# A graph layer with batch norm: z in two banks, tiles held for a late turn, second-stage loads issued later

## The reference

```python
summed = segment_sum(x[src], dst)                 # 50000 x 512
aggr   = summed / max(count, 1)
h      = aggr @ W_l.T + b_l + x @ W_r.T
mu, var = mean(h, axis=0), mean((h - mu)**2, axis=0)
h_norm = relu((h - mu) * rsqrt(var + 1e-5) * gamma + beta)
out    = layernorm(x + h_norm, axis=-1)           # each row, no gain and no bias
```

## Time and profile before

| what | value |
|---|---|
| median of three runs | 2593.97 us (2590.15 to 2595.03) |
| the profiled execution, its own time | 2596.68 us |
| its span in the profile | 2594.9 us |
| busy in the span: PE, DVE, ACT, POOL | 68%, 75%, 57%, 56% |
| moved by DMA | 752.89 MB, a mean of 290 GB/s |

### The profile page before, as it was taken

How to read it: one execution, slowest core, us unless ns; L and a number is a source line. 1 busy time by engine, 2 the same in 40 slices (tenths; PEclk the granted TensorE clock), 3 DMA queues, 4 the chain that set the end, 5 groups by cost and what they waited for, 6 DMA issues and landing times.

```text
span 2594.9 us, 29629 instructions
## 1 busy us (share of the span) xinstructions
PE 1757.6 (68%) x9404; PEld 1415.7 (55%) x9404; DVE 1956.6 (75%) x3451; ACT 1471.8 (57%) x2847; POOL 1456.2 (56%) x700
## 2 busy tenths in 40 slices
PE   7899999999999999999999999996400000000000
PEld 5778778878877887787778778874200000000000
DVE  6745878888877888888788888785688666666666
ACT  4333455545554554454445445542389988888887
POOL 5354555555555555555565555554196655555564
PEclk9999999999999999999999999997755555555555
DMA  5466878887888878888788878877599999999998
GB/s 184 139 211 206 260 250 266 277 253 246 257 263 255 258 246 259 258 255 264 234 262 271 255 243 253 280 240 247 163 410 426 426 426 426 426 412 414 421 421 344
DMA packets 125533, 752.89 MB, mean 290 GB/s; under 512 B 20809, under 2 KB 20809, under 8 KB 65726
## 3 DMA queue, kind: packets, MB, share of 16 engines
q1 hardware_dynamic: 70464, 617.84, 62.1%
q0 software_dynamic: 53664, 132.51, 20.7%
q10 hardware_dynamic: 1246, 0.60, 0.1%
HBM read 515.32 MB, written 246.22 MB: 293 GB/s over the span
## 4 chain that ended last, share of the span: by engine, by line
PE 33%; DMA 32%; issue 9%; DVE 9%; ACT 8%; POOL 7%; SPq 0%; POOLq 0%; ACTq 0%; DVEq 0%
DMA out<-hx 19%; PE pd L524 7%; PE pd L526 7%; PE pd L525 7%; DMA xn<-x,gi 5%; DMA xf<-x,gi 5%; PE pz L627 3%; PE pz L629 3%; PE pz L628 3%; ACT hx L881 3%; POOL xn L1331 2%; ACT hx L891 2%; DVE x_lo L1045 2%; POOL xf L1331 2%; DMA hs<-h_scratch 1%
## 5 line engine op out<-in xcount | busy, mean ns | idle before, releaser
L524 PE MATMUL pd<-wc_hi,x_hi 128*128 128x512 f32 x1564 | 628.8, 402 | 34.8 <-DVE wc_lo L922 17.3
L1379 POOL DMA_INDIRECT h_scratch<-zz,si x156 | 308.8, 1979 | 564.5 <-ACT zz L793 506.9
L735 ACT ACTIVATE h_out<-pd 128x512 f32<-128x512 f32 x391 | 233.6, 597 | 672.3 <-PE pd L526 652.1
L526 PE MATMUL pd<-wc_hi,x_lo 128*128 128x512 f32 x1564 | 614.6, 393 | 0.0
L525 PE MATMUL pd<-wc_lo,x_hi 128*128 128x512 f32 x1564 | 612.9, 392 | 0.0
L1402 POOL TENSOR_TENSOR hx<-hx,scale_b 128x2560 f32<-128x2560 f32 (+2 forms) x91 | 439.4, 4838 | 293.3 <-DMA hx<-h_scratch 251.8
L524 PEld LDWEIGHTS pd<-wc_hi,x_hi 128*128 128x128 f32 x1564 | 295.4, 189 | 98.5 <-issue 29.9
L526 PEld LDWEIGHTS pd<-wc_hi,x_lo 128*128 128x128 f32 x1564 | 295.2, 189 | 64.7
L525 PEld LDWEIGHTS pd<-wc_lo,x_hi 128*128 128x128 f32 x1564 | 295.9, 189 | 57.9
L1331 POOL DMA_INDIRECT xn<-x,gi x156 | 264.9, 1698 | 47.7 <-issue 47.7
L881 ACT ACTIVATE hx<-hx,nm 128x512 f32<-128x512 f32 x391 | 277.1, 710 | 2.8
(11 more groups left out here) (221 smaller groups left out, 2855.0 us busy)
## 6 DMA issues: line engine op xcount, KB each, us to landing
raw<-xT_whole SPq DMA_DIRECT2D x78, 1280.0 KB
h_scratch<-h_out SPq DMA_DIRECT2D x78, 1280.0 KB
hs<-h_scratch SPq DMA_DIRECT2D x78, 1280.0 KB
hx<-x SPq DMA_DIRECT2D x78, 1280.0 KB, 20.7
hx<-h_scratch SPq DMA_DIRECT2D x77, 1280.0 KB, 15.4
out<-hx SPq DMA_DIRECT2D x77, 1280.0 KB, 18.0
xn<-x,gi POOLq DMA_INDIRECT x156
xf<-x,gi POOLq DMA_INDIRECT x156
```

Of the source, the lines that this page charges most:

```text
L524: pe.matmul(pd[i][0:n, :], hi, wc["hi"][:, kc, :], start=kc == 0, stop=False)
L526: last = pe.matmul(pd[i][0:n, :], lo, wc["hi"][:, kc, :], start=False, stop=kc == KC - 1)
L1379: pool.indirect_dma_start(out=h_dram[:, :], out_offset=by, in_=zz[:, h, :], in_offset=None, bounds_check=N + 2 * P - 1, oob_is_err=True, c ...
```

## The change

Five edits, all in the order and the placing of the work. The arithmetic stays the same.

1. **z in two banks.** The second half's product goes to px instead of pz (`z_to`). It no longer waits for ACT's copy of the first half; the next turn's transpose into px waits for the copy of the second half instead.
2. **zz twice.** `zz` gets a second buffer by the turn's parity, and the semaphores of the adds are split by parity (`s_sc[h][b]`). `copy_z` waits for the add of two turns ago; the add of the turn before is now waited for on POOL, in `add_z`.
3. **Four tiles kept.** `tiles_by` spreads 337 tiles over turns 0 to 74 and leaves four, (77,2), (77,3), (77,4) and (78,0), for turn 75 (`HELD = 4`). From turn 75 on POOL issues the gathers of the next turn ahead of the add of the turn before.
4. **The loads of stage two.** None stands in turn 74 any more. Two groups are loaded in turn 77, once all gathers have landed, four more when the last z is summed (`KEPT = 6`), two after `phase_one_done`, the ninth after `bn_ready`. The places of the nine buffers are renumbered so that the first six are free in time.
5. **The order of the sums, and of stage two's first group.** Groups 76 and 77 are read back into `h_out`, which is free by then, so their loads wait for no squares. In turns 78 to 81 DVE takes the sums of a group in front of the squares of the group before. In stage two, group 0 is normalised before group 1 is squared; the other groups keep their order.

```diff
+HELD = 4
-        zz = sr("zz", [P, 2, D], F32)
+        zz = sr("zz", [P, 2, 2, D], F32)
-        KEPT = 3
+        EARLY2, KEPT = 2, 6
+        places = (0, 1, 3, 4, 5, 6, 2, 7, 8)
+        hb = [hx[:, i, 0] for i in places]
+        z_to = (pz, px)
...
-            return min(len(later), TG * EARLY - (TG * EARLY - len(later)) * (u + 1) // (U - REACH))
+            if u >= U - REACH:
+                return len(later)
+            return TG * EARLY + (len(later) - HELD - TG * EARLY) * (u + 1) // (U - REACH)
+        def sums_of(g):
+            return h_out[:, g % 2] if isinstance(g, int) and G - 2 <= g < G else hs[:, g % 2]
...
-                    sp.wait_ge(s_sc[h], 16 * (last + 1))
-                if g >= 2:
-                    sp.wait_ge(s_a2, g - 1)
+                    for v in (last - 1, last):
+                        sp.wait_ge(s_sc[h][v % 2], 16 * (v // 2) + 16)
+                if G - 2 <= g < G:
+                    sp.wait_ge(s_st[0], stored(G))
+                    sp.wait_ge(s_st[1], stored(G - 1))
+                elif g >= 2:
+                    sp.wait_ge(s_a2, g - 1 if g < G else G - 3)
...
                 for u in turns():
                     for g, t in tiles_at(u):
                         if t == tiles_in(g) - 1:
                             after_group(g, g % 2)
-                        if g == G:
-                            load_early()
                     if sums_at(u + 1) is not None:
                         load_sums(sums_at(u + 1))
+                    if u == U - 1:
+                        sp.wait_ge(s_ge, 16 * U)
+                        for h in range(2):
+                            sp.wait_ge(s_gn[h], 16 * U)
+                            sp.wait_ge(s_gf[h], 16 * U)
+                        sp.wait_ge(s_dm, TG * G + 1)
+                        load2(0, EARLY2)
+                sp.wait_ge(s_z, 2 * U)
+                load2(EARLY2, KEPT)
...
# PE, transpose_difference and correction
                     pe.wait_ge(s_dl, 2 * u + h - 1)
+                    if h == 0:
+                        pe.wait_ge(s_ze, 2 * u)
...
-                if 2 * u + h > 0:
-                    pe.wait_ge(s_ze, 2 * u + h)
-                times_wl(pz, P, h).then_inc(s_z, 1)
+                if h == 0 and u > 0:
+                    pe.wait_ge(s_ze, 2 * u - 1)
+                times_wl(z_to[h], P, h).then_inc(s_z, 1)
...
# ACT, copy_z and stage two
-                if u > 0:
-                    act.wait_ge(s_sc[h], 16 * u)
+                if u > 1:
+                    act.wait_ge(s_sc[h][u % 2], 16 * (u // 2))
...
-                if k >= 1 and not by_vector(k - 1):
+                if k == 0:
+                    normalise(0)
+                if k >= 2 and not by_vector(k - 1):
                     normalise(k - 1)
...
# DVE
-                    if sums_at(u - 1) is not None:
+                    if u < U and sums_at(u - 1) is not None:
                         take_squares(sums_at(u - 1))
...
                     if sums_at(u) is not None:
                         take_sums(sums_at(u))
+                    if u >= U:
+                        take_squares(sums_at(u - 1))
...
# POOL
                 def add_z(u, h):
                     pool.wait_ge(s_ze, 2 * u + h + 1)
+                    if u > 0:
+                        pool.wait_ge(s_sc[h][(u - 1) % 2], 16 * ((u - 1) // 2) + 16)
...
-                    if pair_at(u - 1) is not None:
+                    held = u >= U - REACH
+                    if pair_at(u - 1) is not None and not held:
                         add_z(u - 1, 1)
                     if pair_at(u + 1) is not None:
                         gather(u + 1, 0)
                         gather(u + 1, 1)
+                    if pair_at(u - 1) is not None and held:
+                        add_z(u - 1, 1)
```

More of the change, by code:

```diff
@@ L403, in load2_x, with load2 @@
                 sp.dma_start(part_of(xb[i], k), group_of(x, k)).then_inc(s_x2[i], 16)
[L405 to L411 removed]
+            def load2(first, end):
+                for k in range(first, end):
                     load2_h(k)
```

47 lines of the change are left out of this document (21 added, 26 removed).

## The result

| | median, us | runs | ratio to before, 95% interval |
|---|---|---|---|
| before | 2594.21 (2590.15 to 2595.03) | 6 | 1 |
| after | 2575.99 (2571.78 to 2587.80) | 6 | 0.9934 (0.9914 to 0.9954) |

The change makes the kernel 18.2 us faster. The prediction was 43 us, 2551, with a range of 2537 to 2569: the direction is right, the size is not, and the time lies outside the range. The ratio's interval lies clear of 1. The profiled execution of after took 2587.80 us (span 2586.1), 11.8 us over its median and the slowest of the six; that of before stood 2.5 us over its median.

What follows compares the result with a forecast made beforehand. PE was taken to bound stage one's turns, early DMA loads the passage after them, and DMAs stage two from group 1's store. -24 - 19.2 + 0 = -43.2 us gave 2551 us; own range 2541 to 2562, 8 in 10 range 2537 to 2569.

Steps and rivals of the forecast that it cites:

- Part A: Turns 0 to 74, taken as bound by PE: -10.9 - 15.0 + 2 = -24 us.
- the two gains: Turns 0 to 74: four tiles fewer, 10.9 us less; no wait for ACT's copy before the second z, 15.0 less.
- I take off 2 us for that: Turns 0 to 74: allowance for DVE waiting for gathered rows, which have less time in shorter turns; 2 us.
- gathers set the pace: Turns 0 to 74: gathers, not PE, pace the turns, so savings return as PE's waits; 2570 us, 10%.
- Part B: Turn 75 to stage two's start: -16.0, -2.5, -1.2 us for turns 75, 76, 77, then +0.5; together -19.2 us.
- from the last z to the first scaling: End of stage one: faster order of sums eaten by the loads in front; net +0.5 us on 44.7 us.
- SP issues the load of group 75 about 7 us after turn 77 opens: Turn 77: with four loads behind it, transfers of 15.4 us end 9 to 10 us after the last z.
- rival of starved sums: Last sums: loads of groups 76 and 77 delayed by 12 us or more beyond what was set; 2563 us, 10%.
- The row of 10.3 us: Before's add of 74,1, from POOL's end to its load; used to set the last add 10.5 us after last z.
- Part C: Stage two: store of group 0 about 14 us after the start, group 1 unchanged at 31.9; 0, between -3 and +3.
- three signs of being wrong: Turn 75 opens after 1760 us, first scaling after 1850, or group 1's store to end differs from 680 by over 4.
- POOL's new wait: Turns: add wait costs nothing, landings far below 20 us; if it holds the gathers, 2627 us at 1 us excess, 4%.

Runs made afterwards that it cites:

- E6: After with POOL's old order also from turn 75 on, the add of the turn before ahead of the gathers: 2576.61 us, 0.9943 of before.
- E8: After with all early loads of stage two behind the loads for the last sums: 2566.76 us, 0.9899 of before.
- E3: After with DVE's row numbers, indices(u + 2), moved ahead of the additions that take the gathered rows: 2555.08 us, 0.9849 of before.
- E4: Before with DVE's row numbers, indices(u + 2), moved ahead of the additions that take the gathered rows: 2587.84 us, 0.9972 of before.
- E7: After with no tiles kept for turn 75 (HELD = 0): 2575.89 us, 0.9933 of before.
- E2: After with both z in pz again, all other edits kept: 2586.14 us, 0.9970 of before.
- E9: After with the moves of E3 and E8 together: 2550.16 us, 0.9824 of before.
- E12: E9 with both z in pz again: 2559.50 us, 0.9872 of before.
- E11: E9 with DVE's one_hots moved behind the second difference and x_lows(1): 2553.49 us, 0.9843 of before.
- E1: Before with the second z in px and nothing else: 2590.56 us, 0.9990 of before.
- E10: E9 with each of DVE's additions of sums and squares cut in five pieces of one tile: 2551.54 us, 0.9824 of before.

## Why the prediction was wrong, step by step

- **Part A, the two gains: right.** Forecast -10.9 and -15.0 us; the turns at their shortest went down by 26.2.
- **Part A, "I take off 2 us for that": this is the step that failed.** It was right that DVE, waiting for gathered rows, is late next, and the size was taken without working out the loop: the sum of A treats the turns as bound by PE, so that PE's saving is time. The excess rose by 29.3 us in the profile, by 19.0 and 21.5 in E6 and E8, which have the same turns. So part A gave between +3 and -7 us instead of -24. The row that misled is PE's 293.14 of 300 us busy: it was read as "bound by PE". A loop that takes as long as PE's work, give or take a microsecond, looks the same in busy time. What could have been seen is that the means of before's turns (19.61 and 22.48 us) already lay over the shortest ones (19.33 and 21.60), with 17 of 41 five-tile turns over 22.5, and that POOL waited 49.7 us for `si` in 22 turns.
- **The rival "gathers set the pace" was right** and had 10%: it gave 2570, the median is 2576, and E3 shows its mechanism (E4 points the same way). The 6 us between are about what the tail was mis-sized by. What spoke against it, that PE is idle only 2.3%, has no force where both limits are close.
- **Part B, turns 75 to 77: right.** -16.0, -2.5 and -1.2 us forecast, -16.0, -2.1 and -0.4 measured. But the kept tiles and POOL's order play no part that the time shows (E7, E6): what they shift in these turns, the tail takes or gives back.
- **Part B, from the last z to the first scaling: mis-sized**, 51.2 us instead of 45.2. The step that failed is "SP issues the load of group 75 about 7 us after turn 77 opens". It was issued 12.2 us after (1822.41 - 1810.25), and the four loads of stage two stand behind it in SP's program. Counted from the opening of turn 75 the forecast is 39.4 us and the trace has 45.0, with 43.3 to 45.9 in E2, E3, E6 and E7, whatever POOL's order and PE's tiles; in all five the first scaling follows that load by 52.4 to 54.3 us. So the four loads landed until 19 us after the last z, where 9 to 10 stood, and the last add and group 76's load had them alongside. In terms of the sum: POOL was done with the last add 1.0 us later than before (the copy stood behind ACT's squares of group 74), the add took 10.2 us from there where 7.3 were in the sum, the load 7.9 where 5 stood, and the rest went 0.8 faster. E8 shows that the four loads in front do it: without them the tail is 44.4 us. The prediction had allowed for 4 to 6 us of this. Its rival of starved sums (10%) wanted 12 us or more and did not come.
- **The row of 10.3 us was right, its use was not.** The prediction weighed a turn-taking rule from the Trainium skill ("DMA: Bandwidth & Descriptors", section on queues, rings and completion order), with an estimate of 6.4 us for the add, against the trace's 10.3, and said that the sum goes by the trace. The add took 10.2. But 10.5 us after the last z, with POOL done 3.2 us after it in before, is only 7.3 from POOL's end, between the two.
- **Part C: right in each step.** 14.0 and 31.9 us, the dip of the DMA share to 0.00 between, 678.8 to the end (680 +- 4). The groups fetched early bring 3 us at most (E8). Of the three signs of being wrong two came, turn 75 opening at 1777 us and the first scaling at 1875; the third, this time to the end, did not.
- **POOL's new wait: harmless in turns 0 to 74, as forecast, and perhaps not at the end.** It held twice in the span, both times in turn 77 with no gather behind it, ahead of the adds of 76,1 and 77,0:

```profile
1813.63 2.83 POOL L1411 DMA_INDIRECT h_scratch<-zz,si  x1 [2.26 <-DMA h_scratch<-zz,si]
1822.69 2.59 POOL L1411 DMA_INDIRECT h_scratch<-zz,si  x1 [6.22 <-DMA h_scratch<-zz,si]
```

In the 6.22 us ACT's copy of 77,0 was missing too, which ended at 1821.9. The 2.26 us delayed the add whose landing released the load of group 75, so they may be in the tail. No run separates them.

**The sum.** In the profiles part A (+3.1), part B (-11.8), the stretch ahead of turn 0 (+1.4) and stage two (-1.5) make -8.8. In the medians the change is worth 18.2; if part B is worth its 11.8 us in them too, the remaining 6 are what the turns gave in the other executions. That split is argued and not shown: no other execution of after has a profile.

What stays open: the excess of 34 to 48 us that is left in E9 to E12. The waits of E9, E11 and E12 say that a part of it is DVE coming late with `x_lo`, `dd` or `dT_lo`; no run takes it away.

## What to carry to other kernels

Before a saving on a nearly full engine is booked, work out the way round through the other engines (issue, landing, the next step, the next issue) and compare it with that engine's need per turn: where the two differ by less than the saving, book only the difference. Look in an in-order program for work that stands behind a wait it does not need; here two lines moved up were worth 17 to 21 us, the new bank about 10 (alone, in E1, nothing that could be told) and the kept tiles nothing that could be told. And put loads that nobody waits for behind those that somebody does, including behind the adds to memory that these wait for.

## What the runs showed of the hardware

**A gather's issue is held by a long addition on DVE.** An issue that begins during one takes 3.05 against 1.21 us on the mean (after), and 2.96 (E9) falls to 1.59 us (E10) where the addition of 128x2560 is cut in five. The Trainium skill ("SBUF — State Buffer", section on who interferes with whom) says that a DVE instruction with both inputs in SBUF contends with GpSimd instructions that read SBUF, and infers that descriptor generation is spared. The additions have both inputs in SBUF, and here the issue of an indirect DMA is held, so the inference does not hold for these gathers.

**An adding indirect DMA lands late beside plain loads.** 10.2 us from POOL's end to the load it releases with loads of stage two under way (after; 8.5 to 9.6 in E2, E3, E6 and E7), 3.6 us without (E8). How much of it is sharing and how much order between the queues, no run separates.

**The clock can fall after a short idle time.** In after, PE idles 2.33 us for `x_lo` and goes on at half speed:

```profile
1549.31 0.77 PE L546 MATMUL pd<-wc_hi,x_hi 128*128 128x512 f32 x1 [2.33 <-issue]
1549.87 0.63 PE L547 MATMUL pd<-wc_lo,x_hi 128*128 128x512 f32 x1
1550.30 0.63 PE L548 MATMUL pd<-wc_hi,x_lo 128*128 128x512 f32 x1
```

```profile
1549.00:1552.00 3.00, 2.69 (x6) 2.16 (x7) 3.00 (x3) 0.00 (x0) 0.34 (x1) 0.50 1.06 302
```

The matmuls start 0.43 us apart instead of 0.23, and the granted clock is 0.50, the lower of the two levels (1.2 GHz). Of the nine idle times of 1.9 us and more in turns 0 to 74 of after, six were followed by such matmuls within about 1 us; behind the other three (1.90, 2.04 and 2.33 us long) the granted clock stayed 1.00. In turns 0 to 74, 47 matmuls started 0.43 us apart in after and 22 in before, which is 9.4 and 4.4 us on top of the waits: a wait of PE can cost more than its length.
